# The first graph layer's linear part: whole-layer loads, two accumulators of each kind, bn_stats norm across strips, and the split on ACT and POOL

## The reference

```python
def _layernorm(x, axis=-1, eps=1e-05):
    m = jnp.mean(x, axis=axis, keepdims=True)
    v = jnp.var(x, axis=axis, keepdims=True)
    return (x - m) / jnp.sqrt(v + eps)

def _L0_gnn_ref(h, edge_src, edge_dst, edge_val, W1, b1, W2, b2, eps):
    neigh = jax.ops.segment_sum(h[edge_src] * edge_val[:, None], edge_dst, num_segments=N_NODES)
    x = (1.0 + eps) * h + neigh
    x = jax.nn.relu(x @ W1 + b1)
    x = x @ W2 + b2
    return jax.nn.relu(x)
...
x = _layernorm(x + _L0_gnn_ref(x, src, dst, edge_weight, ...), axis=-1)
x = _layernorm(x + _L1_gnn_ref(x, edge_index, ...), axis=-1)
```

## Time and profile before

| what | us |
|---|---|
| median of 3 runs (lowest, highest) | 2071.18 (2070.48, 2072.76) |
| the profiled execution, its own time | 2069.24 |
| span of its trace | 2067.4 |
| `gin_nodes`, from SP's first load to SP's first load of the next stage | 477.20 to 543.69: 66.49 |

### The profile page before, as it was taken

The page is one execution under the profiler, slowest core; times in us unless marked ns, Lnnn a source line. Parts: engine busy times, 40 slices in busy tenths (PEclk is TensorE's granted clock), DMA queues, the critical chain, the costliest instruction groups (busy, mean ns, idle before and its releaser), DMA issues. The chain is left out here.

```text
span 2067.4 us, 56651 instructions
## 1 busy us (share of the span) xinstructions
PE 1640.1 (79%) x23014; PEld 1482.0 (72%) x23014; DVE 1481.0 (72%) x2364; ACT 1232.5 (60%) x1981; POOL 886.1 (43%) x559
## 2 busy tenths in 40 slices
PE   4599999964388882378888888881499799999996
PEld 1599999953376761377778777771499788898895
DVE  6788989834577774389999999984688644444545
ACT  1355666521255551298889988881367566666665
POOL 0699999801445542098888877700000000000000
PEclk9799999986699996589999999995799999999998
DMA  1100000002111211311110011103300000000001
GB/s 57 41 14 13 15 14 13 14 7 80 52 34 50 55 52 29 76 32 42 43 42 27 22 42 43 38 3 103 97 26 13 24 20 12 3 1 3 16 1 52
DMA packets 82632, 68.24 MB, mean 33 GB/s; under 512 B 21630, under 2 KB 74001, under 8 KB 82273
## 3 DMA queue, kind: packets, MB, share of 16 engines
q1 hardware_dynamic: 79047, 62.01, 10.4%
q0 software_dynamic: 3328, 2.56, 0.7%
HBM read 47.36 MB, written 17.19 MB: 31 GB/s over the span
## 5 line engine op out<-in xcount | busy, mean ns | idle before, releaser
L2251 ACT ACTIVATE branch_mask<-branch_row,att_att 128x3126 bf16<-128x3126 f32 (+1 forms) x208 | 461.0, 2289 | 46.5 <-DMA branch_row<-dst_row 38.7
L2564 PE MATMUL sage_acc<-sage_cr,sage_hl 128*128 128x448 f32 x1750 | 378.5, 372 | 10.3 <-DVE sage_hl L2680 10.3
L497 POOL DMA_INDIRECT swp_slab<-records,e_rows x100 | 314.4, 3144 | 89.7 <-POOLq L120 55.9
L2564 PEld LDWEIGHTS sage_acc<-sage_cr,sage_hl 128*128 128x128 f32 x1750 | 324.1, 189 | 35.7 <-DVE sage_hl L2680 10.4
L2328 PE MATMUL branch_acc<-branch_v,branch_mask 128*128 128x102 bf16 (+1 forms) x5000 | 299.7, 214 | 61.9 <-DVE branch_mask L2278 37.5
L2284 DVE TENSOR_TENSOR branch_mask<-branch_mask,k_C 128x3126 bf16<-128x3126 bf16 (+1 forms) x208 | 312.6, 1550 | 17.2 <-ACT branch_mask L2251 16.3
L2590 ACT ACTIVATE sage_cr<-k_C 128x896 fp32r<-128x896 bf16 x250 | 235.2, 945 | 146.8 <-PE sage_acc L2564 142.7
L2328 PEld LDWEIGHTS branch_acc<-branch_v,branch_mask 128*128 128x128 bf16 (+1 forms) x5000 | 256.7, 100 | 87.9 <-DVE branch_mask L2278 41.5
L2650 DVE CAST sage_cr<-k_C 128x896 fp32r<-128x896 bf16 x250 | 128.6, 515 | 207.2 <-PE sage_acc L2564 207.2
L2517 POOL TENSOR_TENSOR sage_xr<-sage_xr,sage_b 128x640 f32<-128x640 f32 x5 | 7.7, 1551 | 470.4 <-DMA sage_xr<-x 470.4
L419 PE MATMUL swp_pw<-swp_hot,swp_low_hot 128*128 128x100 bf16 x1568 | 198.9, 217 | 12.9 <-DVE swp_hot L413 9.8
(11 more groups left out here) (297 smaller groups left out, 2902.4 us busy)
## 6 DMA issues: line engine op xcount, KB each, us to landing
branch_row<-dst_row SPq DMA_DIRECT2D x24, 384.0 KB
mean_feat<-in_edge_attr SPq DMA_DIRECT2D x50, 144.0 KB, 2.2
branch_row<-dst_row SPq DMA_DIRECT2D x8, 411.0 KB
table<-lin_tab SPq DMA_DIRECT2D x5, 340.0 KB, 5.9
branch_tab<-table SPq DMA_DIRECT2D x8, 212.5 KB
att_sums<-branch_mask SPq DMA_DIRECT2D x8, 212.5 KB, 2.3
post_sums<-att_sums SPq DMA_DIRECT2D x5, 340.0 KB, 3.2
table<-lin_tab SPq DMA_DIRECT2D x5, 322.5 KB, 2.4
```

Of the source, the lines that this page charges most:

```text
L497: pool.indirect_dma_start(slab[:, t % 2, j * ROW:(j + 1) * ROW, :].rearrange("p e f -> p (e f)"), None, k.records, bass.IndirectOffsetOnAx ...
L2251: nc.scalar.activation(mask[:, slot(e, s), cols(lo, hi)], row[:, cols(lo, hi)], ACT.Relu, bias=g.att[:, 1, bass.ds(h + s * heads, 1)], sca ...
L2564: ins = pe.matmul(acc[:, bank, 0:hi - lo], hl[:, part, g % RING, :], cr[:, n % CR_SLOTS, lo - first:hi - first], start=g == 0 and part == ...
```

## The change

Only `gin_nodes` is changed, and `split_strip` goes. What it does:

- `x` and `vT` hold all 25 tiles. SP issues all ten loads at once behind the constants, features and rows by turns, each strip with a semaphore of its own. The five stores follow.
- Each of the four constants has its own semaphore, and is waited for where it is first used.
- `pH` and `pO` have two buffers each. PE runs the first product one strip ahead: first(i+1), then second(i). The wait for `hT` and for DVE (`taken`) is for the strip two back.
- The hidden activation is written over `vT`, the second layer's sum over that again (`y`), and the residual and the normed rows over `x`.
- DVE does the norm by `bn_stats` and `bn_aggr` for each tile, one addition of epsilon, a reciprocal, and for each tile one `tensor_scalar` that subtracts the mean and multiplies. Its order is residual(0), residual(1), norm(0), residual(2), norm(1) and so on, with `wait_ge(normed, ...)` ahead of the later residuals.
- ACT does the two casts of the split (`high`, `middle`), POOL the two subtractions (`lower`, `low`).

```diff
-        x, vT = m.sb("x", [P, 2, STRIP, D], F32), m.sb("vT", [P, 2, SW], F32)
-        y, sq, out, rest = (m.sb(n, [P, STRIP, D], F32) for n in ("y", "sq", "out", "rest"))
-        hT = m.sb("hT", [P, SW], F32)
-        pH, pO = (m.ps(n, [P, 2 * BANK]) for n in ("pH", "pO"))
+        x, vT = m.sb("x", [P, TILES, D], F32), m.sb("vT", [P, NP], F32)
+        rest = m.sb("rest", [P, STRIP, D], F32)
+        stats, mv = m.sb("stats", [P, STRIP, 6], F32), m.sb("mv", [P, 2, STRIP, 2], F32)
+        st = m.sb("st", [P, 2, 2, STRIP], F32)
+        pH, pO = (m.ps(n, [P, 2, 2 * BANK]) for n in ("pH", "pO"))
...
                 for i in range(STRIPS):
-                    if i + 2 < STRIPS:
-                        sp.wait_ge(h_ready, i + 1)
-                        load_v(i + 2)
-                        sp.wait_ge(added, i + 1)
-                        load_x(i + 2)
+                    if i:
+                        sp.dma_start(nodes(i), k.vT[:, i * SW:(i + 1) * SW]).then_inc(v_in[i], 16)
+                    sp.dma_start(x[:, tiles(i), :], strip_of(a["x"], i)).then_inc(x_in[i], 16)
+                for i in range(STRIPS):
                     sp.wait_ge(normed, i + 1)
...
             @block.gpsimd
             def _(pool):
                 for i in range(STRIPS):
-                    pool.wait_ge(normed, i + 1)
-                    split_strip(pool, split, out, rest, parts, i)
+                    pool.wait_ge(high, i + 1)
+                    if i:
+                        pool.wait_ge(low, i)
+                    pool.tensor_tensor(rest[:, :, :], x[:, tiles(i), :], parts[:, 0, tiles(i), :],
+                                       ALU.subtract).then_inc(lower, 1)
+                    pool.wait_ge(middle, i + 1)
+                    pool.tensor_tensor(parts[:, 2, tiles(i), :], rest[:, :, :], parts[:, 1, tiles(i), :],
+                                       ALU.subtract).then_inc(low, 1)
...
+                def residual(i):
+                    y = nodes(i).rearrange("p (t f) -> p t f", f=D)
                     dve.wait_ge(o_ready, i + 1)
...
+                    dve.tensor_tensor(y, pO[:, i % 2, 0:SW].rearrange("p (t f) -> p t f", f=D),
+                                      mid(b2[:, :], STRIP), ALU.add).then_inc(taken, 1)
+                    dve.wait_ge(taken, i + 1)
+                    dve.wait_ge(x_in[i], 16)
+                    link(dve.scalar_tensor_tensor(out=x[:, tiles(i), :], in0=y, scalar=0.0,
+                                                  in1=x[:, tiles(i), :], op0=ALU.max, op1=ALU.add))
+                    for c in range(STRIP):
+                        ins = dve.bn_stats(stats[:, c, :], x[:, i * STRIP + c, :])
+                    ins.then_inc(counted, 1)
+                    dve.wait_ge(counted, i + 1)
+                    for c in range(STRIP):
+                        ins = dve.bn_aggr(mv[:, i % 2, c, :], stats[:, c, :])
+                    link(ins)
+                    dve.tensor_scalar(st[:, i % 2, 0, :], mv[:, i % 2, :, 1], LN_EPS, None, ALU.add).then_inc(var, 1)
+
+                def norm(i):
+                    dve.wait_ge(std, i + 1)
+                    link(dve.reciprocal(st[:, i % 2, 1, :], st[:, i % 2, 1, :]))
+                    for c in range(STRIP):
+                        t = i * STRIP + c
+                        ins = dve.tensor_scalar(x[:, t, :], x[:, t, :], mv[:, i % 2, c, 0:1], st[:, i % 2, 1, c:c + 1],
+                                                ALU.subtract, ALU.mult)
+                    ins.then_inc(normed, 1)
...
+                residual(0)
                 for i in range(STRIPS):
-                    finish(i)
+                    if i + 1 < STRIPS:
+                        residual(i + 1)
+                    norm(i)
+                    if i + 2 < STRIPS:
+                        dve.wait_ge(normed, i + 1)
...
             @block.scalar
...
                 hidden(0)
+                hidden(1)
+                spread(0)
+                for i in range(STRIPS):
+                    if i + 2 < STRIPS:
+                        hidden(i + 2)
+                    if i + 1 < STRIPS:
+                        spread(i + 1)
+                    act.wait_ge(normed, i + 1)
+                    nc.scalar.activation(parts[:, 0, tiles(i), :], x[:, tiles(i), :], ACT.Copy).then_inc(high, 1)
+                    act.wait_ge(lower, i + 1)
+                    nc.scalar.activation(parts[:, 1, tiles(i), :], rest[:, :, :], ACT.Copy).then_inc(middle, 1)
...
             @block.tensor
...
+                def first(i):
+                    pe.wait_ge(v_in[i], 16)
+                    if i > 1:
+                        pe.wait_ge(hT_ready, i - 1)
...
+                first(0)
                 for i in range(STRIPS):
                     if i + 1 < STRIPS:
-                        hidden(i + 1)
...
+                        first(i + 1)
                     pe.wait_ge(hT_ready, i + 1)
+                    if i == 0:
+                        pe.wait_ge(w2_in, 16)
+                    if i > 1:
+                        pe.wait_ge(taken, i - 1)
```

More of the change, by code:

```diff
@@ L798, in gin_nodes, with tiles, nodes @@
         m = Memory(nc, ctx, "gin")
-        w1, w2 = m.sb("w1", [P, D], F32), m.sb("w2", [P, D], F32)
-        b1, b2 = m.sb("b1", [P, 1], F32), m.sb("b2", [P, D], F32)
-        x, vT = m.sb("x", [P, 2, STRIP, D], F32), m.sb("vT", [P, 2, SW], F32)
-        y, sq, out, rest = (m.sb(n, [P, STRIP, D], F32) for n in ("y", "sq", "out", "rest"))
-        hT = m.sb("hT", [P, SW], F32)
-        st = m.sb("st", [P, 3, STRIP], F32)
-        pH, pO = (m.ps(n, [P, 2 * BANK]) for n in ("pH", "pO"))
-        consts = m.sem("consts")
-        x_in, v_in = ([m.sem(f"{n}{s}") for s in (0, 1)] for n in ("x_in", "v_in"))
-        h_ready, hT_ready, o_ready, added = m.sem("h_ready"), m.sem("hT_ready"), m.sem("o_ready"), m.sem("added")
-        var, std = m.sem("var"), m.sem("std")
-        chain, normed, stored, split = (m.sem(n) for n in ("chain", "normed", "stored", "split"))
+        x, vT = m.sb("x", [P, TILES, D], F32), m.sb("vT", [P, NP], F32)
[3 more added lines that the diff above has]
+        pH, pO = (m.ps(n, [P, 2, 2 * BANK]) for n in ("pH", "pO"))
+        w1, w2, b2 = (m.sb(n, [P, D], F32) for n in ("w1", "w2", "b2"))
+        b1 = m.sb("b1", [P, 1], F32)
+        w1_in, b1_in, w2_in, b2_in = (m.sem(n) for n in ("w1_in", "b1_in", "w2_in", "b2_in"))
+        x_in, v_in = ([m.sem(f"{n}{s}") for s in range(STRIPS)] for n in ("x_in", "v_in"))
+        h_ready, hT_ready, o_ready, taken = m.sem("h_ready"), m.sem("hT_ready"), m.sem("o_ready"), m.sem("taken")
+        counted, var, std, chain, normed, stored = (
+            m.sem(n) for n in ("counted", "var", "std", "chain", "normed", "stored"))
+        high, lower, middle, low = (m.sem(n) for n in ("high", "lower", "middle", "low"))
+        def tiles(i):
+            return slice(i * STRIP, (i + 1) * STRIP)
+        def nodes(i):
+            return vT[:, i * SW:(i + 1) * SW]
         with nc.Block() as block:
@@ L845, in _ @@
             @block.vector
             def _(dve):
[L847 to L848 removed]
+                link = Chain(dve, chain)
+                def residual(i):
+                    y = nodes(i).rearrange("p (t f) -> p t f", f=D)
                     dve.wait_ge(o_ready, i + 1)
[L850 to L865 removed]
@@ new lines, in _ @@
+            @block.tensor
+            def _(pe):
+                pe.wait_ge(w1_in, 16)
+                def first(i):
+                    pe.wait_ge(v_in[i], 16)
+                    if i > 1:
+                        pe.wait_ge(hT_ready, i - 1)
+                    for lo, hi in halves(SW):
+                        ins = pe.matmul(pH[:, i % 2, lo:hi], w1[:, :], vT[:, i * SW + lo:i * SW + hi],
+                                        start=True, stop=True)
+                    ins.then_inc(h_ready, 1)
+                first(0)
@@ L882, in _ @@
                 for i in range(STRIPS):
                     if i + 1 < STRIPS:
-                        hidden(i + 1)
-                    act.wait_ge(var, i + 1)
-                    nc.scalar.activation(st[:, 2, :], st[:, 1, :], ACT.Sqrt).then_inc(std, 1)
-            @block.tensor
-            def _(pe):
-                pe.wait_ge(consts, 16 * 4)
-                for i in range(STRIPS):
-                    pe.wait_ge(v_in[i % 2], (i // 2 + 1) * 16)
-                    if i:
-                        pe.wait_ge(hT_ready, i)
-                    for lo, hi in halves(SW):
-                        ins = pe.matmul(pH[:, lo:hi], w1[:, :], vT[:, i % 2, lo:hi], start=True, stop=True)
-                    ins.then_inc(h_ready, 1)
+                        first(i + 1)
```

62 lines of the change are left out of this document (14 added, 48 removed).

## The result

| | before | changed | ratio (95% interval) |
|---|---|---|---|
| first job, median (lowest, highest), us | 2071.38 (2070.48, 2075.92), 5 runs | 2058.98 (2049.46, 2059.61), 5 runs | 0.9919 (0.9896, 0.9943) |
| second job | 2071.47 (2066.86, 2073.76), 19 runs | 2056.46 (2053.33, 2059.84), 4 runs | 0.9931 (0.9910, 0.9952) |
| third job | 2069.94 (2064.66, 2076.86), 11 runs | 2055.74 (2052.24, 2062.01), 6 runs | 0.9931 (0.9910, 0.9952) |

The changed kernel is 0.7 to 0.8% faster, 12.4 to 15.0 us by the medians; the forecast was 14.6 us and 2056.6 us. Both kernels spread over 5 to 12 us from run to run. A job is one batch of runs; its kernels are compared with the same runs of the kernel before. The profiled execution of the changed kernel took 2059.61 us, with a span of 2057.5.

A forecast was written before the change was run, and what follows sets the result against it. The bound was gin_nodes, where DVE and POOL hand one strip back and forth. Start 490.5 plus 3.35, 1.6, 5.0, three periods of 6.4, 3.0 and 5.4 gave 528.1, before 542.72: 14.6 us gained, 2056.6, range 2051 to 2061.5.

The forecast's parts named there:

- R0: Time at which DVE can begin its first addition in gin_nodes: 490.5, bounds 489.5 and 491.5, against 490.12 before.
- DVE's work: DVE's uncontended time per strip in gin_nodes: residual 3.35 us and norm 1.66, together 5.0, against about 7.2 before.
- The stall of the second strip: DVE waits 1.6 us after residual(0), while PE does first(2) and second(1) in 4.9 us at clock 0.5.
- nothing collides, and PE's clock is full: Rival: both POOL subtractions slip under bn_stats, no stall, period 5.1; 20 us gained, 2051; chance 0.14.
- if L856 waits for PE or for ACT in each strip: Sign of being wrong: DVE's addition waits each strip, as when an ACT cast ahead of a relu holds up second.
- The collision: One of POOL's two subtractions per strip stops DVE, costing 1.4 us, bounds 0 and 2.8; period 6.4.
- twice: Rival: both POOL subtractions are paid by DVE each strip, period 7.8; 9 us gained, 2062; chance 0.09.
- 7.2: Time DVE's eight norm and two residual instructions needed per strip before, from 7.17 us busy in ten.
- Norm(4) and the tail: Stage's end: norm(4) 3.0 us with one subtraction stopping it, then POOL and ACT finish the split in 5.4.
- Late loads: Rival: loads flow at only 98 GB/s, so residual(4) waits; 12.5 us gained, 2058.7; chance 0.09.
- The step from the stage to the whole: Claim that every row behind gin_nodes shifts by the stage's 14.6 us, giving the whole 2056.6 us.
- the clock behind the stage: Rival "slower": TensorE's lower clock in the next stage costs more than 14.6 us, whole 2075 or more; chance 0.03.

The follow-up runs named there:

- kernel with POOL's casts: The changed kernel with the split's two casts given back from ACT to POOL: stage 51.92 us against 49.3, whole 2053.65 us in one run.

## Why the prediction was right, and where not

The median (2056.6 forecast; 2058.98, 2056.46 and 2055.74 measured) and the sign were right, and the mechanism is the forecast one. But two errors stand in it that nearly cancel, and that the median was met within 2.4 us is in part luck: the stage gained 17.2 us, not 14.6, and part of it, some 3 us by the medians, did not arrive. The 2.6 us of the stage are the stall (1.6), three periods (18.58 us for 19.2) and norm(4) (0.4).

- *The start.* R0 was forecast 13.3 us into the stage and was 13.19. PE began earlier than said (3.26 us into the stage, not some 5.5), and it was of no use, since first(1) had to wait for its features, forecast 8.3 and measured 8.59.
- *DVE's work.* Residual 3.35: 3.38. Residual and norm 5.0: 498.39 - 493.41 = 4.98. The rows of the last layer carried over to this stage as they were.
- *The stall of the second strip* was the largest wrong term, 1.6 us forecast and 0 measured. I took PE's clock at its lower level, from the mean of 0.66 of a later stretch. But PE had worked without a pause from 485.43, and from 489.75 the clock was at the upper level. The trace of the kernel before had it already, at the place in question, where the first product of strip 2 takes half of 2.50:

```profile
493.82 1.25 PE L896 MATMUL gin_pH<-gin_vT,gin_w 128*128 128x512 f32 x4
```

The rival "nothing collides, and PE's clock is full" was right on the clock here, but not in the later strips, whose second products took 2.50 again.
- *The wait that was named as a sign of being wrong*, "if L856 waits for PE or for ACT in each strip", did come in two strips, through the very cast ahead of a relu that the prediction names: 0.16 us each, so small that the sum bears it. The kernel with POOL's casts, where no cast stands on ACT, has no such wait.
- *The collision.* 1.4 a strip forecast; measured once a strip, as said, 1.08 in the strip shown (1.90 for 0.82) and 1.2 in strip 2 (2.03). With the wait for PE that makes a period of 6.2. POOL was first, by 0.17 us in the strip shown. It was the right trace to read, the port row in the last layer. The Trainium skill, "SBUF — State Buffer", "Who interferes with whom", calls the shared port pair an exclusive lock and says that issue order decides who blocks. L860 needed 0.67 us after POOL's end, for 0.82 without POOL, which agrees but for 0.15. What the prediction has from the same place on tensor_reduce, no run here tests. The rival "twice" did not come true in the changed kernel, but its mechanism did in the last norm of the kernel with POOL's casts (4.71).
- *Two counts beside the sum.* The "7.2" us of DVE's ten instructions before is busy time within ten microseconds and holds the 1.2 us in which L855 stood; without them and the 2.18 a strip took 6.9. And seven DVE instructions of a strip can be stopped, not six: the small tensor_scalar is one of them, by the prediction's own.
- *Norm(4) and the tail.* 3.0 and 5.4 forecast, 2.58 (516.97 to 519.55) and 5.67 measured. ACT's cast takes 0.74, for 0.78.
- *Late loads.* They did not come late; DVE never waited for rows.
- *The step from the stage to the whole* was the wrong one in kind: "behind it every row shifted by the same 14.6 us". The next stage began 17.6 us earlier and the first store 9.9 us earlier in the traced executions. The rival for it, the clock behind the stage, was priced only as something that turns the result round, and at 0.03. Behind the stage the three traces of the changed kernel are 2.5 to 7.7 us longer than before; that the clock is the cause is likely, and not shown. Nor did the range know of the spread of the runs: three runs before had stood within 2.3 us, and 19 later ones within 7.

## What to carry to other kernels

Where DVE and POOL both work on SBUF data, count the instructions that can be stopped (two SBUF inputs, tensor_scalar) and see under which instructions the other engine's work falls: here it was 1.1 us of a period of 6.2. bn_stats isn't stopped, so a subtraction that falls under it costs DVE nothing; how the old norm would have fared in the new order was not run. In a pipeline that runs one engine a strip ahead and another a strip behind, keep the loads free of the stores' waits: here, on one engine that issues both in order, the old order cost 15.4 us. Where several engines hand work to and fro, follow the round as well as each engine's own work: here they were 0.3 us apart. And read what a part is worth from its stage in the trace, within 0.7 us, since the whole moves by several microseconds of its own.

## What the runs showed that was not expected

The spread from run to run was 5 to 12 us (2064.66 to 2076.86 for the kernel before in one job), though the first three runs stood within 2.3. Behind the stage, where the code is the same in all kernels, PE's busy time varies between 1219 and 1231 us. Part of the spread lies ahead of the stage, where the code is the same as well: in the fourteen traces it began between 474.00 and 478.00 us. The Trainium skill, "TensorE: Matmul & The Clock Gate", "What's actually happening", says that the number of products at the lower clock at a kernel's start differs from run to run, and puts the cost of that ramp below 1% of a usual span. Here the spread is 0.3 to 0.6%, and in the two traced stretches above the clock's column differs too, in the middle of the kernel; that the ramp makes the spread is not shown.
